# A state-space and mixture-of-experts kernel: other orders of work on every engine in the first stage

## The reference

```python
x1 = x + mamba(ctx, z=layernorm(x))
out = x1 + moe(layernorm(x1))

def mamba(hidden, z):                 # 512 channels, 16 states
    x = in_proj(hidden)               # (batch, 512 channels, 512 steps)
    x = silu(causal_conv4(x) + conv_b)                        # u
    dt_low, B, C = split(x_proj(x), 16, 16, 16)
    dt = softplus(dt_proj(dt_low) + dt_b)
    state = state * exp(dt * A) + (dt * x) * B   # step by step
    y = sum over states of state * C
    return (y + D * x) * silu(z)

def moe(x):                           # 16 experts, 2 used, one shared
    ...
```

## Time and profile before

| | |
|---|---|
| median of 3 runs | 1047.64 us (1046.64 to 1052.21) |
| the profiled execution, its own time | 1049.27 us |
| span of the profiled execution | 1047.5 us |
| mean granted TensorE clock | 0.932 |
| busy: TensorE, VectorE, GpSimd, ScalarE | 895.6, 828.7, 753.4, 517.6 us |
| first scan of VectorE, the end of the first stage's path | 105.62 us |

### The profile page before, as it was taken

How to read it: one execution, slowest core, us unless ns; L and a number is a source line. 1 busy time by engine, 2 the same in 40 slices (tenths; PEclk the granted TensorE clock), 3 DMA queues, 4 the chain that set the end, 5 groups by cost and what they waited for, 6 DMA issues and landing times.

```text
span 1047.5 us, 16598 instructions
## 1 busy us (share of the span) xinstructions
PE 895.6 (85%) x4352; PEld 650.5 (62%) x4353; DVE 828.7 (79%) x1349; ACT 517.6 (49%) x959; POOL 753.4 (72%) x482
## 2 busy tenths in 40 slices
PE   5886555779999889988999999889999999998994
PEld 1222334556665556655656555659988888997993
DVE  4788899999999799999999525876798978989000
ACT  3777734455655465555555222125554544554551
POOL 2436899889999799989994111038878788887873
PEclk9987656789999999999999989989999999999997
DMA  5568912552228422562210320145777766674432
GB/s 175 194 255 301 360 53 89 203 211 89 81 64 311 149 80 68 199 245 90 77 62 11 136 78 20 30 166 147 192 201 199 205 183 191 176 222 111 80 60 41
DMA packets 69987, 152.14 MB, mean 145 GB/s; under 512 B 7585, under 2 KB 23969, under 8 KB 64306
## 3 DMA queue, kind: packets, MB, share of 16 engines
q1 hardware_dynamic: 59410, 126.97, 35.0%
q0 software_dynamic: 10528, 24.65, 11.9%
HBM read 112.80 MB, written 38.80 MB: 145 GB/s over the span
## 4 chain that ended last, share of the span: by engine, by line
PE 40%; DVE 31%; issue 18%; DMA 4%; ACT 3%; POOL 2%; DVEq 1%; SPq 0%; ACTq 0%; POOLq 0%
DVE bank L1347 8%; PE bank L665 7%; PE bank L769 6%; DVE gs L1361 6%; PE bank L771 6%; PE bank L770 6%; PE bank L684 6%; PE bank L611 3%; DVE p_acc L1289 2%; DVE e_gu_lo L1478 2%; DVE h_p L1347 2%; PE bank L573 2%; DVE e_gu_hi L1477 1%; DMA xt<-x_scratch 1%; PE bank L758 1%
## 5 line engine op out<-in xcount | busy, mean ns | idle before, releaser
L1154 POOL TENSOR_TENSOR dbu<-bcs,m_w 128x2048 f32<-128x2048 f32 x64 | 296.2, 4630 | 10.0 <-DVE bank L1347 7.1
L925 ACT ACTIVATE bank<-m_dt,c_a 128x512 f32<-128x512 f32 x256 | 171.0, 686 | 197.5 <-DVE gs L1361 197.4
L1347 DVE TENSOR_TENSOR_SCAN bank<-bank,dbu 128x512 f32<-128x512 f32 x192 | 229.8, 1218 | 13.8 <-ACT bank L925 9.3
L665 PE MATMUL bank<-ws_gu,f_xnT 128*128 128x352 f32 x576 | 194.6, 480 | 2.0 <-ACT f_hT L947 2.0
L611 PE MATMUL bank<-ident,gs 128*128 128x128 f32 x768 | 133.1, 303 | 70.4 <-DVE gs L1361 62.2
L611 PEld LDWEIGHTS bank<-ident,gs 128*128 128x128 f32 x768 | 94.0, 152 | 128.0 <-DVE gs L1361 103.8
L665 PEld LDWEIGHTS bank<-ws_gu,f_xnT 128*128 128x128 f32 x576 | 108.1, 199 | 49.9 <-issue 7.4
L769 PE MATMUL bank<-e_gu_hi,e_xT_hi 128*128 x376 | 129.5, 344 | 7.1 <-POOL e_xT_lo L1219 4.6
L1361 DVE TENSOR_TENSOR gs<-bank,bcs 128x512 f32<-128x512 f32 x192 | 127.7, 672 | 0.0
L771 PE MATMUL bank<-e_gu_hi,e_xT_lo 128*128 x376 | 121.4, 323 | 0.0
L770 PE MATMUL bank<-e_gu_lo,e_xT_hi 128*128 x376 | 121.4, 323 | 0.0
(11 more groups left out here) (166 smaller groups left out, 1676.5 us busy)
## 6 DMA issues: line engine op xcount, KB each, us to landing
bcs<-bc_scratch SPq DMA_DIRECT2D x32, 1024.0 KB, 8.9
e_gu<-in_wgu SPq DMA_DIRECT2D x16, 1408.0 KB, 9.1
e_dn<-in_wdn SPq DMA_DIRECT2D x16, 512.0 KB, 4.3
out_rows<-xt SPq DMA_DIRECT2D x18, 256.0 KB, 2.1
p_x<-in_x SPq DMA_DIRECT2D x4, 1024.0 KB, 6.8
u_scratch<-p_u SPq DMA_DIRECT2D x4, 1024.0 KB, 3.9
silu_z_scratch<-p_sz SPq DMA_DIRECT2D x4, 1024.0 KB, 5.0
dt_scratch<-p_dt SPq DMA_DIRECT2D x4, 1024.0 KB, 4.3
```

The lines of the kernel that those rows point to most:

```text
L665: last = mm(dst[:, 0:I], lhs[t], ws_gu[:, t, off:off + I], start=t == 0, stop=t == KH - 1)
L925: f(HS[k % RING_H][:], m_dt[:, q % 2, :], ACT.Exp, scale=c_a[:, q, n:n + 1]).then_inc(exp_done, 1)
L1154: g.tensor_tensor(part_, Bs[:, gr * GRP:(gr + 1) * GRP, :], w, ALU.mult).then_inc(dbu_ready, 1)
L1347: v.tensor_tensor_scan(to, h, dbu[:, n, :], 0.0, ALU.mult, ALU.add).then_inc(scan_done, 1)
```

## The change

It reorders the first stage on every engine.

- SP: `p_in` is loaded in two halves (quarters 0 and 1 ahead of the context, 2 and 3 behind it).
- ScalarE: one small silu on a constant runs before the first convolution. In each iteration `silu_u` of quarter 0 is followed by the convolution of quarter 0 and then the others. `conv_again(b + 1, 3)` moves from between the exps to between the logs. Batch 3 has its u before its z, and the first decay waits for 15 silus of z by semaphore.
- TensorE: `x_in(b + 1, 2)` follows `x_dbl` directly; the turned rows stand between the four `dt_in`; `x_in(b + 1, 3)` follows them. In the last batch turns 1 and 2 go to banks 0 and 1.
- VectorE: the statistics of batch 0 follow all four quarters of taps. Those of batch b + 1 come first in an iteration (second in batch 0). `taps(b + 1, 3)` moves from behind the first soft to between the second and third gap.

```diff
--- before.py
+++ after.py
@@ -91,7 +91,7 @@
 
         bank = [stack.enter_context(nc.psum_tensor(f"bank{i}", [P, 512], F32)) for i in range(8)]
         XIN, XDB, DTP = bank[0:2], bank[2], bank[4:8]
-        SZT = ((bank[3], bank[3], bank[2], bank[3]), (bank[3], bank[2], bank[3], bank[2]))
+        SZT = ((bank[3], bank[3], bank[2], bank[3]), (bank[3], bank[0], bank[1], bank[3]))
         HS, Y, GU, YO, TP = bank[0:3], bank[3], bank[4:6], bank[6], bank[7]
         G, U = GU
         LG = YO[:, 0:NE]
@@ -353,8 +353,10 @@
                 sp.dma_start(m_x[:, par], batch_rows(x, b)[:, :, q * P:(q + 1) * P]).then_inc(x_loaded[par], 16)
                 sp.dma_start(m_szT[:, par, :], sz_d[bass.ds(b, 1), :, q, :].rearrange("a p l -> p (a l)")).then_inc(s_loaded[par], 16)
 
+            in_rows = inT.rearrange("(t p) n -> p t n", p=P)
+            sp.dma_start(p_in[:, :, 0:2 * P], in_rows[:, :, 0:2 * P]).then_inc(in_loaded, 16)
             load_ctx(0)
-            sp.dma_start(p_in[:], inT.rearrange("(t p) n -> p t n", p=P)).then_inc(in_loaded, 16)
+            sp.dma_start(p_in[:, :, 2 * P:H], in_rows[:, :, 2 * P:H]).then_inc(in_loaded, 16)
             for dst, src in ((c_conv[:], convw), (c_convb[:], convb)):
                 sp.dma_start(dst, src).then_inc(conv_loaded, 16)
             sp.dma_start(p_x[0][:], batch_rows(x, 0)).then_inc(z_loaded[0], 16)
@@ -548,6 +550,8 @@
             def x_in(b, q):
                 if q == 0:
                     pe.wait_ge(ctx_loaded, b * 16 + 16)
+                if b == 0 and q == 2:
+                    pe.wait_ge(in_loaded, 32)
                 wait(pe, conv_done, b * DT + q - 1)
                 for t in range(2):
                     last = mm(XIN[q % 2][:], p_in[:, t, q * P:(q + 1) * P], p_ctx[b % 2][:, t, :], start=t == 0, stop=t == 1)
@@ -558,16 +562,18 @@
                 final = b == B - 1
                 if q == 0:
                     wait(pe, sz_ready, b * TB)
-                elif q == (1 if final else 2):
-                    pe.wait_ge(xd_copied, b + (not final))
+                elif final and q < 3:
+                    pe.wait_ge(conv_done, b * DT + q + 2)
+                elif q == 2:
+                    pe.wait_ge(xd_copied, b + 1)
                 else:
-                    pe.wait_ge(sz_ready, b * TB + ((0, 1, 0, 2), (0, 0, 1, 2))[final][q])
+                    pe.wait_ge(sz_ready, b * TB + (1 if final else (0, 1, 0, 2)[q]))
                 for t in range(TB):
                     last = nc.tensor.transpose(SZT[final][q][:, t * P:(t + 1) * P], p_x[b % 2][:, q, t * P:(t + 1) * P], ident[:])
                 last.then_inc(z_turned, 1)
 
             def x_dbl(b):
-                wait(pe, sz_ready, b * TB + TB * (b == B - 1))
+                wait(pe, sz_ready, b * TB)
                 for q in range(DT):
                     pe.wait_ge(u_ready, b * DT + q + 1)
                     last = mm(XDB[0:NX, :], p_xp[:, q, :], p_u[:, q, :], start=q == 0, stop=q == DT - 1)
@@ -585,17 +591,20 @@
             pe.wait_ge(consts_made, 7)
             pe.wait_ge(const_loaded, 16 * 7)
             for b in range(B - 1):
-                z_turn(b, 0)
+                if b:
+                    z_turn(b, 0)
                 x_dbl(b)
+                x_in(b + 1, 2)
+                if b == 0:
+                    z_turn(b, 0)
+                dt_in(b, 0)
                 z_turn(b, 1)
-                x_in(b + 1, 2)
-                dt_in(b, 0)
+                dt_in(b, 1)
                 z_turn(b, 2)
+                dt_in(b, 2)
                 z_turn(b, 3)
-                dt_in(b, 1)
+                dt_in(b, 3)
                 x_in(b + 1, 3)
-                dt_in(b, 2)
-                dt_in(b, 3)
                 if b < B - 2:
                     x_in(b + 2, 0)
                     x_in(b + 2, 1)
@@ -855,11 +864,11 @@
                 act.wait_ge(u_ready, (b - 1) * DT + q + 1)
                 conv_first(b, q)
 
-            def silu_u(b):
-                wait(act, u_stored, b * 16)
-                for q in range(DT):
-                    act.wait_ge(conv_done, b * DT + q + 1)
-                    f(p_u[:, q, :], p_acc[:, q, :], ACT.Silu).then_inc(u_ready, 1)
+            def silu_u(b, q):
+                if q == 0:
+                    wait(act, u_stored, b * 16)
+                act.wait_ge(conv_done, b * DT + q + 1)
+                f(p_u[:, q, :], p_acc[:, q, :], ACT.Silu).then_inc(u_ready, 1)
 
             def silu_z(b, q):
                 if q == 0:
@@ -879,35 +888,42 @@
                 act.wait_ge(abs_done, b * DT + q + 1)
                 f(p_e[:, q, :], p_e[:, q, :], ACT.Exp, scale=-1.0).then_inc(e_ready, 1)
 
-            def logs(b):
-                for q in range(DT):
-                    act.wait_ge(wm_ready, b * DT + q + 1)
-                    f(p_e[:, q, :], DTP[q][:], ACT.Ln, bias=1.0).then_inc(ln_ready, 1)
-
+            def log(b, q):
+                act.wait_ge(wm_ready, b * DT + q + 1)
+                f(p_e[:, q, :], DTP[q][:], ACT.Ln, bias=1.0).then_inc(ln_ready, 1)
+
+            act.wait_ge(consts_made, 2)
+            f(p_rs[:], halves[:], ACT.Silu)
             for q in range(DT):
                 conv_first(0, q)
             for b in range(B - 1):
-                silu_u(b)
+                silu_u(b, 0)
                 conv_again(b + 1, 0)
+                for q in range(1, DT):
+                    silu_u(b, q)
                 conv_again(b + 1, 1)
-                silu_z(b, 0)
+                if b:
+                    silu_z(b, 0)
                 xd_copy(b)
-                silu_z(b, 1)
                 conv_again(b + 1, 2)
-                silu_z(b, 2)
-                silu_z(b, 3)
+                for q in range(b > 0, TB):
+                    silu_z(b, q)
                 if b == 0:
                     act.wait_ge(const_loaded, 16 * 7)
                     f(c_a[:], c_alog[:], ACT.Exp).then_inc(a_exp, 1)
-                exps(b, 0)
+                for q in range(DT):
+                    exps(b, q)
+                log(b, 0)
+                log(b, 1)
                 conv_again(b + 1, 3)
-                for q in range(1, DT):
-                    exps(b, q)
-                logs(b)
+                log(b, 2)
+                log(b, 3)
+            for q in range(DT):
+                silu_u(B - 1, q)
             for q in range(TB):
                 silu_z(B - 1, q)
-            silu_u(B - 1)
             act.wait_ge(a_ready, 1)
+            act.wait_ge(sz_ready, B * TB - 1)
 
             def decay(b, q, n):
 
@@ -975,7 +991,8 @@
                     if first and n in EXPS_AT:
                         exps(B - 1, EXPS_AT.index(n))
                     if first and n == LOGS_AT:
-                        logs(B - 1)
+                        for k in range(DT):
+                            log(B - 1, k)
                     if rows and n == ADD_AT:
                         row_out(j)
                     if rows and n == LOGITS_AT:
@@ -1307,28 +1324,30 @@
                 dve.wait_ge(gap_ready, b * DT + q + 1)
                 v.scalar_tensor_tensor(p_dt[:, q, :], DTP[q][:], 0.0, p_dt[:, q, :], ALU.min, ALU.add).then_inc(dt_ready, 1)
 
-            taps(0, 0)
-            taps(0, 1)
+            for q in range(DT):
+                taps(0, q)
             z_stats(0)
-            taps(0, 2)
-            taps(0, 3)
             for b in range(B - 1):
+                if b:
+                    z_stats(b + 1)
                 taps(b + 1, 0)
                 if b:
                     for q in range(DT):
                         total(b - 1, q)
+                else:
+                    z_stats(1)
                 taps(b + 1, 1)
                 taps(b + 1, 2)
-                z_stats(b + 1)
-                soft(b, 0)
-                taps(b + 1, 3)
-                for q in range(1, DT):
+                for q in range(DT):
                     soft(b, q)
                 if b == 0:
                     dve.wait_ge(a_exp, 1)
                     v.tensor_scalar(c_a[:], c_a[:], -1.0, None, ALU.mult).then_inc(a_ready, 1)
-                for q in range(DT):
-                    gap(b, q)
+                gap(b, 0)
+                gap(b, 1)
+                taps(b + 1, 3)
+                gap(b, 2)
+                gap(b, 3)
             for q in range(DT):
                 total(B - 2, q)
```

## The result

The changed kernel took 1052.35 us as the median of 22 runs (1049.83 to 1056.58), the kernel before 1048.16 us (1044.27 to 1052.76). The ratio is 1.0033, with a 95% interval of 1.0019 to 1.0048: 3.5 us slower (2.0 to 5.0), inside what I called "no change" by my bound of 0.5%. The median lies inside the range. Against the forecast of + 1.3 us, the ratio's + 3.5 is 2.2 us more.

A forecast was written before the change was run, and what follows sets the result against it. VectorE bounds the scan stage, a chain the stage before it. Terms reach +1.8 us at the last silu of u, -0.9 tail, +0.4 x_dbl(3): +1.3 us, forecast median 1049 us ("no change"), range 1043.5 to 1055.5.

The forecast's parts named there:

- Start: First product and taps: halved load gains 0.75 us, TensorE starts at 5.5, first taps at 10.25 in place of 12.31.
- The term for the table: ScalarE's first table load leaves the path ahead of the first taps: 1.3 us gained, with no further drain.
- Batch 0: Statistics behind the taps: x_dbl(0) ends at 25.65; batch 1's silu of u starts at 45.25, 3.05 us earlier.
- E to T: Middle batches, end of product x_dbl (E) to start of next silu of u (T): 18.5 us, before 18.0.
- T to E: Start of silu of u (T) to end of x_dbl (E), batches 1 and 2: 9.45 and 8.2 us, before 7.35 and 6.1.
- The tail: Last batch, silu of u to first scan: 6.6 us in place of 7.5, 0.9 us gained.
- The tie: Before the first scan, GpSimd's dbu ready at 107.7 at the latest against ScalarE's 106.5: costs 1.2 us at most.
- x_dbl(3): Last batch's x_dbl now stands behind turn 3: some 0.4 us later seen from the first scan.
- Signs of being wrong: x_dbl of batches 1 or 2 at 3.6 us, first scan before 101 or after 111, VectorE under 95% busy, dbu last.
- clock stays high: Rival: TensorE keeps 2.4 GHz over its 7 us gap, 2.2 us less in each of two batches, 1044.5 us; chance 0.13.
- VectorE as the bound: Rival: batches run at VectorE's own 22 us, first scan about 97.5, 8 to 9 us faster, 1039 us; chance 0.09.
- The slowest rival: Turns between dt products keep TensorE's clock low, 4.8 us in each of three batches, 1063.3 us; chance 0.02.

The follow-up runs named there:

- experiment 4: Changed kernel plus 7 extra TensorE products ahead of x_in(b + 2, 1) in batches 1 and 2, 20 small ones in the last: ratio 0.998 to the kernel before, 1046.96 us.
- experiment 3: Changed kernel with the input weights loaded whole, behind the context, as before: ratio 1.003 to the kernel before.
- experiment 6: Changed kernel with TensorE's old order behind x_dbl in batches 1 and 2, plus 5 extra products a batch and 20 small at the end: ratio 0.9921, 1042.27 us.
- experiment 7: Kernel of experiment 6 with dt and u of slot (0, 0) loaded ahead of batch 2's silu(z) store: ratio 0.9941 to the kernel before, 1042.25 us.
- experiment 9: Changed kernel with the statistics of batch 0 put back between the taps: ratio 1.0066 to the kernel before, 1056.56 us.
- experiment 5: Changed kernel with TensorE's old order behind x_dbl and silu(z) 1's old place in batches 1 and 2, batch 0 partly altered: ratio 0.9989, 1046.72 us.
- experiment 1: Changed kernel with the next batch's last convolution quarter put back on ScalarE and VectorE: ratio 1.0076 to the kernel before, 1056.93 us.
- experiment 2: Kernel of experiment 1 with TensorE's x_in(b + 1, 3) moved ahead of dt_in(b, 3): ratio 1.0004 to the kernel before.
- experiment 8: The kernel before with 4 extra TensorE products ahead of x_dbl in batches 1 and 2, nothing else: ratio 1.0002.

## Why the prediction was right, and where it was off

- **The bound** was right: the first scan moved by 3.0 and the third by 3.8 us, and the time by 3.5.
- **Start** (forecast: TensorE at 5.5, taps at 10.25): the load gave 0.3 us in place of "I take 0.75", by seven profiles against six. The term for the table held at the first taps: they begin 4.7 us behind TensorE's start (6.05 before). The profiled execution of the changed kernel started 1.1 us late.
- **Batch 0** (T at 45.25): 46.88 in that execution, 45.82 in the one of experiment 4, which has the same batch 0 and started at 5.76. From TensorE's start that is 39.9 and 40.1 us; the forecast had 39.75. In experiments 3, 6 and 7, also with this batch 0, it is 41.3 to 41.4: the clock fell before the last turn, E to T took 20.6 to 21.3 us in place of 19.8, and in 3 and 6 the first products were slower too. So the forecast holds by its steps where the clock stays high, and the profiled execution was lucky in this as it was unlucky in its start. The forecast had no term for the fall. VectorE's wait was called about 3 us and is 5.08; the prediction's own schedule gives nearly 5 (statistics over near 27.7, row four at 32.5). I called z_stats(1)'s wait a hold of what follows; experiment 9 shows that it cost nothing.
- **E to T** (18.5): 18.83 and 18.69. Experiment 5 shows the named cause, silu(z) behind the turns. It gave 2.5 us back, more than the 0.5 us that I set against the kernel before, since with the softs in their new place the old turns are faster than either order.
- **T to E** (9.45 and 8.2): 9.33 and 7.78. Taps(b + 1, 3) ended at the next T (75.14 against 75.04), and experiment 4 shows the clock as the cause. The gap of TensorE was forecast at 7 us and was 4.70 and 4.17: the two products ahead of it, partly at the low clock, took 5.91 us and ended at E + 14.8, not at E + 11.2.
- **VectorE's new order** in itself was no loss: experiments 1 and 2 put the quarter back and E to T rose to between 20.5 and 23 us.
- **The tail** (6.6): 7.1. The tie that I gave 1.2 us at most went to GpSimd: it waited for u until 102.61, and dbu was ready last (3.43 us of VectorE's idle time ended by it). Experiment 7 removed it. The mis-sized term is the time from the silu(z) store at 90.31 to the data, 12.3 us. My bound for it was 13.3, with some 2 us less if the data had waited.
- **x_dbl(3)** (0.4 us): 0.8. It ran 6.21 us, with 0.58 of its clock from 105.3 to 111.5.
- **The sum**: the profiled first scan is 2.1 us later than forecast, 1.6 of it by T of batch 1 (1.1 the late start of that execution), 0.5 in the tail; the third scan 0.4 more. In the time it is 2.2 us. The late start is one execution's and no part of that. The mis-sized terms that the runs name are the load, the tail and x_dbl(3), 1.3 us together, and batch 0, where the five profiles with its order lie 1.0 us above the forecast on the mean, counted from the start. By my estimate from these rows that makes 2.3; the interval of the time, 2.0 to 5.0 us, is too wide to test it.
- **Signs of being wrong**: two of those that I had named did appear, and the forecast held all the same. x_dbl of batch 1 took 3.63 us: the low clock had fallen on the product and the turn ahead of it, which cost the same in sum. And dbu came last. VectorE was busy 96.7% behind the first scan (185.15 of 191.38 us to 300).
- **Of the rivals**, "clock stays high" is excluded by the 0.50 window; VectorE as the bound came true only once both the turns and the clock were put right (experiment 6). The slowest rival was partly there: the clock did fall in the mixed stretch of dt products and turns. In batches 1 and 2 of the changed kernel it cost 0.1 us at most, since the last turn ran before or just at the fall and x_in(b + 1, 3), 3.8 us in place of 2.0, is needed only some 3 us later. Where the fall came earlier, it cost: 0.8 to 1.5 us in batch 0 of experiments 3, 6 and 7, 1.3 us in batch 2 of experiment 1. That is this rival at a fraction of the 4.8 us a batch that I gave it. In experiment 1, which needs the product early, ScalarE waited 2.75 us. The rule of the Trainium skill (TensorE: Matmul & The Clock Gate, Part 4: PE-mode transpose), that a transpose does not count as busy work of the engine in the same way, fits this fall better than I gave it credit for; but dt products with 17 rows were mixed in, and no run tells the two apart.

## What to carry to other kernels

Reordering four engines at once moves the work that others queue behind: for each moved piece ask what is late because of it on the next engine, and how long that engine will have been idle, since here TensorE came back at 1.2 GHz after 4 to 5 us without work and the chain paid twice. A low clock or a long wait is worth removing only where the chain runs through it: extra products took 2 us off the first scan in one order (the earlier start left out), and in the other nothing that a kernel without them did not show too. And a large idle time in front of one instruction (5 us of VectorE in batch 0) can be free; what the next engine does meanwhile (here ScalarE, without a wait) says so, and an experiment on that place confirms it.

## What the runs showed of the hardware that was not expected

TensorE's granted clock fell to 1.2 GHz while it was busy without a break: 0.55 from 62.4 to 66 in the changed kernel, where turns of 128 by 128 and dt products of 17 rows alternate, and 1.00 in the same stretch of the kernel before, where a full product stands among them (61.00; 62.42 in experiment 5). Over all profiles, this fall shows in each of the twelve batches 1 and 2 with the changed order (dt products at up to 2.07 us in place of 1.12, or the product behind at 3.6 to 3.8 in place of 2.0), and in one of the sixteen with the old order (experiment 8, 58.57). So the order matters, but a full product in between did not always keep the clock up. TensorE's start with the same order of loads varied from 5.73 to 6.97 us between executions, more than the change of the order was worth. The load of u took 9.4 us from issue to use behind the silu(z) store and its neighbours (93.19 to 102.61), and 5.3 us (80.85 to 86.19) once it stood ahead of them.
